# Attention scores with 32 keys in four column tiles, turned by VectorE in 32x32 blocks

## What is computed

```python
scores = einsum('bshc,btc->bsht', q_nope, kv) + einsum('bshr,btr->bsht', q_pe, k_pe)   # 128 + 64 features
scores = softmax(scores / sqrt(192) + causal_mask)       # over the 64 keys t
out = einsum('bsht,btc->bshc', scores, kv)               # kv: 128 features
x = x + out @ (wkv_b, wo folded, per head) + wo_b
```

## Time and profile before

| | |
|---|---|
| median of 3 runs | 1075.35 us (1074.99 to 1075.48) |
| the profiled execution's span | 1073.7 us |
| PE busy | 1052.0 us (98%), mean granted clock 0.999 |
| DVE, ACT, POOL busy | 501.7, 340.6, 280.1 us |
| where stage m's units lie in the span | first scores at 190.6 us, last at 641.1 us |

### The profile page before, as it was taken

One profiled execution on the slowest core, in us unless ns is written; L12 is line 12 of the kernel. 1 busy time (PEld: TensorE's weight loads), 2 busy tenths in 40 slices (PEclk: granted clock), 3 DMA queues, 4 the chain that ended last, 5 costly groups with the idle time before them and its releaser, 6 DMA issues.

```text
span 1073.7 us, 16794 instructions
## 1 busy us (share of the span) xinstructions
PE 1052.0 (98%) x6465; PEld 862.3 (80%) x6465; DVE 501.7 (47%) x914; ACT 340.6 (32%) x630; POOL 280.1 (26%) x329
## 2 busy tenths in 40 slices
PE   6999999999999999999999999999999999999997
PEld 3677786788888888888888888888888888888886
DVE  3666556545555544555555557442522251234114
ACT  3565545423222232123222234342222222223220
POOL 2433362321112111131111312232242123213412
PEclk9999999999999999999999999999999999999999
DMA  9999973200022000220013061600020002000101
GB/s 361 415 418 396 386 274 91 72 20 21 21 64 94 20 12 21 72 96 21 20 50 99 21 206 41 216 1 1 1 76 4 1 1 79 1 1 1 40 1 40
DMA packets 40755, 101.24 MB, mean 94 GB/s; under 512 B 6954, under 2 KB 11077, under 8 KB 36197
## 3 DMA queue, kind: packets, MB, share of 16 engines
q1 hardware_dynamic: 38948, 96.62, 25.3%
q10 hardware_dynamic: 1728, 3.54, 0.8%
HBM read 74.45 MB, written 17.30 MB: 85 GB/s over the span
## 4 chain that ended last, share of the span: by engine, by line
PE 96%; DVE 1%; issue 1%; DMA 1%; POOL 0%; ACT 0%; SPq 0%; DVEq 0%; POOLq 0%; ACTq 0%
PE b_z L44 8%; PE b_z L46 8%; PE b_z L45 8%; PE b_turn L44 5%; PE b_turn L46 4%; PE b_turn L45 4%; PE b_score L44 4%; PE b_score L46 4%; PE b_prob L46 4%; PE b_prob L44 4%; PE b_score L45 4%; PE b_prob L45 4%; PE b_read L46 4%; PE b_read L44 4%; PE b_read L45 4%; PE b_read L623 2%
## 5 line engine op out<-in xcount | busy, mean ns | idle before, releaser
L1516 POOL TENSOR_TENSOR f_hT_lo<-f_h,f_hT_hi 128x512 fp32r<-128x512 f32 x64 | 82.1, 1283 | 241.3 <-ACT f_hT_hi L1571 232.3
L1632 DVE TENSOR_TENSOR f_h<-f_h 128x512 f32<-128x512 f32 x64 | 45.4, 710 | 154.8 <-ACT f_h L1564 154.8
L816 POOL TENSOR_TENSOR m_sc<-m_sc,m_rs 128x1024 f32<-128x1024 f32 x16 | 30.5, 1908 | 248.5 <-DVE m_rs L979 248.5
L44 PE MATMUL b_z<-m_zT_lo,m_wq_hi 128*128 128x512 f32 x192 | 74.9, 390 | 0.3 <-issue 0.3
L46 PE MATMUL b_z<-m_zT_hi,m_wq_hi 128*128 128x512 f32 x192 | 74.7, 389 | 0.0
L45 PE MATMUL b_z<-m_zT_hi,m_wq_lo 128*128 128x512 f32 x192 | 74.7, 389 | 0.0
L987 DVE TENSOR_TENSOR m_x<-b_score,m_x 128x512 f32<-128x512 f32 x32 | 22.1, 691 | 97.3 <-PE b_score L46 97.3
L858 ACT ACTIVATE m_qT<-b_z,m_q_bias 128x512 f32<-128x512 f32 x64 | 44.1, 689 | 71.1 <-PE b_z L46 65.2
L806 POOL TENSOR_TENSOR m_qpe<-m_qpe,m_swapped 128x512 f32<-128x512 f32 x32 | 41.3, 1292 | 79.7 <-DMA m_swapped<-m_by_sin 79.7
L1571 ACT CAST f_hT_hi<-f_h 128x512 fp32r<-128x512 f32 x64 | 39.8, 622 | 52.4 <-DVE f_h L1632 52.4
L879 ACT ACTIVATE m_sc<-m_sc 128x512 f32<-128x512 f32 x32 | 20.2, 632 | 103.0 <-DVE m_sc L971 103.0
(11 more groups left out here) (280 smaller groups left out, 2863.9 us busy)
## 6 DMA issues: line engine op xcount, KB each, us to landing
x_ctx_in<-ctx_rows_dram SPq DMA_DIRECT2D x16, 1024.0 KB, 14.5
x_ctxT<-ctx_turned_dram SPq DMA_DIRECT2D x15, 1024.0 KB, 14.0
m_swapped<-m_by_sin SPq DMA_DIRECT2D x128, 64.0 KB, 2.0
m_raw<-attn_raw_dram SPq DMA_DIRECT2D x6, 768.0 KB, 10.6
m_z_in<-z_scratch SPq DMA_DIRECT2D x4, 1152.0 KB, 5.7
x_x_all<-x_dram SPq DMA_DIRECT2D x16, 256.0 KB, 14.7
m_x<-x_scratch SPq DMA_DIRECT2D x4, 1024.0 KB, 6.3
x_scratch<-m_x SPq DMA_DIRECT2D x4, 1024.0 KB, 4.3
```

The source lines that it names most:

```text
L44: nc.tensor.matmul(out, lh, rl, start=first, stop=False)
L816: q.tensor_tensor(e, e, rs[:].unsqueeze(2).broadcast_to([P, HB, SEQ]), ALU.mult).then_inc(s["normed"], 1)
L1516: q.tensor_tensor(hT_lo[k % 6][:], h[:, k % 2], hT_hi[k % 6][:].bitcast(F32), ALU.subtract).then_inc(s["h_lo"], 1)
L1632: v.tensor_tensor(h[:, k % 2], h[:, k % 2], h[:, k % 2], ALU.mult).then_inc(s["squared"], 1)
```

## The change

Scores are computed for 32 keys at a time in four column tiles of 32 columns, with 128 moving columns where the keys are the first half of a sequence (k = 0) and 64 where they are the second half (k = 1): the first half of the queries sees none of those keys, and this quarter is left out. Tokens are placed so that partition 32c + i of tile t holds token 128c + 32t + i of the group. PE's transposes of scores and of probabilities go; VectorE transposes 32x32 blocks instead, out of PSUM for the scores and from SBUF to SBUF for the probabilities. The mask moves to GpSimd, behind the turn. The maximum and the sum are taken over 32 keys and then joined over the two halves, by two small instructions each. `weigh` has four row tiles of 32 keys, with 256 or 128 moving columns. Loads and stores of latents and residual rows are cut in four, one for each quadrant of partitions.

```diff
     def load_z(sp, g):
-        sp.dma_start(z_in[:, :, 0:ZW], z_t[g]).then_inc(z_loaded, 16)
-        sp.dma_start(z_in[:, :, ZW:ZW + ROPE], z_t[g][:, :, QLR + KVLR:ZW]).then_inc(z_loaded, 16)
+        for c in range(PARTS):
+            sp.dma_start(z_in[part(c), :, 0:ZW], z_t[g, c]).then_inc(z_loaded, 16)
+            sp.dma_start(z_in[part(c), :, ZW:ZW + ROPE], z_t[g, c][:, :, QLR + KVLR:ZW]).then_inc(z_loaded, 16)
...
         def store_x2(g):
             sp.wait_ge(s["x2_done"], T4 * UNITS * (g + 1))
-            sp.dma_start(x2_t[g], x1[:]).then_inc(s["x2_stored"], 16)
+            for c in range(PARTS):
+                sp.dma_start(x2_t[g, c], x1[part(c)]).then_inc(s["x2_stored"], 16)
...
         def load_x1(g):
-            sp.dma_start(x1[:], x1_t[g]).then_inc(s["x1_loaded"], 16)
+            for c in range(PARTS):
+                sp.dma_start(x1[part(c)], x1_t[g, c]).then_inc(s["x1_loaded"], 16)
...
+        def mask(u):
+
+            pool.wait_ge(s["s_turned"], 2 * (u + 1))
+            own = sc[:].rearrange("p (b w n) -> p b w n", b=2, w=3)[:, :, 0::2]
+            q.tensor_tensor(own, own, causal[:].unsqueeze(1).unsqueeze(1).broadcast_to([P, 2, 2, HU * QB]),
+                            ALU.add).then_inc(s["masked"], 1)
...
         def slot(g, n, u):
             if runs(g, n, 1):
+                mask(u - 1)
+            rope_add(u, 0)
+            if runs(g, n, 1):
                 norm(u - 1)
-            rope_add(u)
+            rope_add(u, 1)
             if n == 1:
                 bias_x1(g)
...
+        def turn_scores(u):
 
             dve.wait_ge(s["scored"], u + 1)
+            to = sc[:].rearrange("p (w n) -> p w n", w=6)
             for h in range(2):
+                v.transpose(to[:, :, P // 2 * h:P // 2 * h + P // 2],
+                            b_s[h][:, 0:3 * P].rearrange("p (w n) -> p w n", w=6)).then_inc(s["s_turned"], 1)
+
+        def turn_probs(u):
+
+            dve.wait_ge(s["normed"], u + 1)
+            dve.wait_ge(s["pv"], u)
+            v.transpose(pT[:], sc[:]).then_inc(s["p_turned"], 1)
+
+        def over_keys(u, own, both, op, done, behind):
+
+            v.tensor_reduce(both[:].rearrange("p b w h -> p (b w h)"), sc[:].rearrange("p (n k) -> p n k", k=QB), AX_X, op).then_inc(s[done], 1)
+            dve.wait_ge(s[done], u + 1)
+            v.tensor_copy(own[:, :, 0], both[:, :, 0]).then_inc(s[behind], 1)
+            v.tensor_tensor(own[:, :, 1:3], both[:, :, 1].unsqueeze(2).broadcast_to([P, 2, 2, HU]),
+                            both[:, :, 2].unsqueeze(2).broadcast_to([P, 2, 2, HU]), op).then_inc(s[behind], 1)
 
         def shift(u):
 
+            dve.wait_ge(s["masked"], u + 1)
+            over_keys(u, mx, tops, ALU.max, "maxed", "topped")
+            dve.wait_ge(s["topped"], 2 * (u + 1))
...
             if runs(g, n, 1):
                 shift(u - 1)
+            rotate(n, u, 1)
+            if runs(g, n, 1):
                 invert(u - 1)
-            rotate(n, u, 1)
...
+            if runs(g, n, 1):
+                turn_probs(u - 1)
+                probs(u - 1)
             add(0)
...
+            pe.wait_ge(s["pT_lo"], u + 1)
+            for b in range(2):
                 for n, (kv, p) in enumerate(((kv_hi, pT_lo), (kv_lo, pT_hi), (kv_hi, pT_hi))):
+                    for k in range(2):
+                        cols = slice(2 * P * b + P * k, 2 * P * b + 2 * P)
+                        of = slice(3 * P * b + 2 * P * k, 3 * P * b + 2 * P + P * k)
+                        for c in range(PARTS):
+                            mm = t_.matmul(b_o[c][:, cols], kv[part(c), 2 * b + k], p[part(c), of],
+                                           start=n == 0 and k == 0, stop=n == 2 and k == 1)
...
+            for b in range(2):
+                for k in range(2):
+                    for h in range(2):
+                        for c in range(PARTS):
+                            t_.matmul(b_s[h][part(c), cols(b, k)], keys_all[:, 0, 2 * b + k, c], queries(qT[:, h::2], b, k, c),
+                                      start=b == 0 and k == 0, stop=False)
+            for b in range(2):
+                for k in range(2):
+                    for h in range(2):
+                        for c in range(PARTS):
+                            of = slice(SEQ * h, SEQ * h + SEQ)
+                            mm = t_.matmul(b_s[h][part(c), cols(b, k)], keys_all[of, 1, 2 * b + k, c], queries(qpe[of], b, k, c),
+                                           start=False, stop=b == 1 and k == 1)
```

More of the change, by code:

```diff
@@ L691, in stage_m @@
     by_sin, swapped = low("by_sin", [P, TT]), low("swapped", [P, TT])
-    cos, sin = low("cos", [P, SEQ]), low("sin", [P, SEQ])
-    HB = T4 * HU
-    mx, es, rs = low("mx", [P, HB]), low("es", [P, HB]), low("rs", [P, HB])
+    cos, sin = low("cos", [P, 2 * P]), low("sin", [P, 2 * P])
+    tops, mx, adds, es, rs = (low(n, [P, 2, 3, HU]) for n in "tops mx adds es rs".split())
     x1 = sb("x1", [P, T4, HID])
@@ L795, in gpsimd @@
         pool.wait_ge(s["setup"], 1)
[L796 to L806, removed]
+        for c in range(PARTS):
+            rows = causal[part(c)].rearrange("p (h k) -> p h k", k=QB)
+            q.affine_select(out=rows, in_=rows, compare_op=ALU.is_ge, fill=-BIG, base=0,
+                            pattern=[[0, HU], [-1, QB]], channel_multiplier=1).then_inc(s["consts"], 1)
@@ L827, in groups @@
             slots(pool, slot)
-        return dict(groups=groups, rope_add=rope_add, norm=norm)
+        return dict(groups=groups, rope_add=rope_add, mask=mask, norm=norm)
     def scalar(act):
@@ L861, in probs @@
         def probs(u):
[L862 to L865, removed]
+            act.wait_ge(s["p_turned"], u + 1)
+            act.wait_ge(s["pv"], u)
+            a.copy(pT_hi[:], pT[:]).then_inc(s["pT_hi"], 1)
         def out(u):
@@ L869, in out @@
             act.wait_ge(s["projected"], T4 * u)
[L870 to L873, removed]
+            for c in (2, 3, 0, 1):
+                a.copy(of_part(oT_hi, c), b_o[c][:].rearrange("p (t h q) -> p t h q", t=T4, h=HU)).then_inc(s["oT_hi"], 1)
         def exp(u):
[L877 to L880, removed]
+            act.wait_ge(s["shifted"], u + 1)
+            a.activation(sc[:], sc[:], ACT.Exp, scale=SCALE).then_inc(s["exped"], 1)
         def slot(g, n, u, values_hi):
@@ L1024, in slot @@
                 out(u - 1, 1)
-            mask(u)
+            turn_scores(u)
             if runs(g, n, 1):
@@ L1037, in tables @@
             dve.wait_ge(s["tables"], 48)
-            dve.wait_ge(s["consts"], 2)
+            dve.wait_ge(s["consts"], PARTS)
         return dict(latent=latent, groups=groups, rotate=rotate, invert=invert, probs=probs, out=out,
-                    mask=mask, shift=shift, residual=residual, tables=tables)
+                    turn_scores=turn_scores, turn_probs=turn_probs, shift=shift, residual=residual, tables=tables)
     def tensor(pe):
@@ L1080, in rope_half @@
             mm.then_inc(s["rope_made"], 1)
-        def turn_scores(u):
-            pe.wait_ge(s["masked"], 2 * (u + 1))
-            for half in range(2):
-                turn(b_s[half], lambda k: sc[:, HALF * half + P * k:HALF * half + P * k + P], HB // 4).then_inc(s["s_turned"], 1)
         def q_unit(g, n, u):
@@ L1120, in project, with weigh @@
             mm.then_inc(s["projected"], 1)
-        def weigh(g, u, half, last=False):
+        def weigh(g, u, last=False):
             pe.wait_ge(s["kv_lo"], g + 1)
@@ L1182, in slot @@
                 turn_latent(g + 1, 1)
-            if runs(g, n, 1):
-                turn_probs(u - 1)
             if head and u == 1:
@@ L1195, in slot @@
                     pe.wait_ge(s["zq_lo"], T4 * (g + 2))
-                for half in range(2):
-                    weigh(before(1)[0], u - 1, half)
+                weigh(before(1)[0], u - 1)
             scores(g, u)
@@ L1987, in _ @@
             m["out"](U - 1, 1)
-            m["mask"](U)
+            m["turn_scores"](U)
             m["out"](U - 1, 0)
@@ L2065, in _ @@
             pe.wait_ge(F["s"]["xT_lo"], 4)
-            for half in range(2):
-                m["weigh"](G, U - 1, half)
+            m["weigh"](G, U - 1)
             m["scores"](G, U)
-            m["project"](2, U - 1, 0)
-            m["turn_scores"](U)
-            for i in range(1, 4):
+            for i in range(3):
                 m["project"](2, U - 1, i)
             f["up"](0, 0)
-            m["turn_probs"](U)
             f["up"](0, 1)
-            m["weigh"](G, U, 0, last=True)
+            m["project"](2, U - 1, 3)
             pe.wait_ge(F["s"]["relu"], 2)
-            m["weigh"](G, U, 1, last=True)
+            m["weigh"](G, U, last=True)
             f["up"](0, 2)
```

165 lines of the change are left out of this document (74 added, 91 removed).

## The result

The changed kernel takes 1105.07 us, the median of four runs (1104.57 to 1107.51), beside 1075.41 for the kernel before on the same chip: a ratio of 1.028 (95% interval 1.0266 to 1.0295), 29.7 us slower. 11.6 were forecast. The profiled execution has a span of 1102.8 us, 29.1 more than before.

What follows compares the result with a forecast made beforehand. PE, busy 98% of the span, was taken as the bound. Terms -28.2 - 10.1 + 0 + 33.4 + 6 + 8.1 + 2.4 = 11.6 us more gave 1085.3 profiled, 1087.0 median; own range 1073 to 1101, whole range 1064 to 1111.

Steps and rivals of the forecast that it cites:

- group 0's stop: PE in group 0, slot n=1, behind the late swap DMAs: about 1 us, since there are no project tiles yet.
- PE's stream: PE's own work over 16 units: 38.3 us shorter, 28.2 from turns removed and 10.1 from scores.
- the scores: Score matmuls on PE: 2.30 us a unit for 2.93 if tiles stay independent, 0.63 less, 10.1 in all.
- the weighing: PE's weigh matmuls: no change taken; bounds 5.9 us less or 9.3 more in all.
- The long stops: Slot n=2, groups 1 to 3: PE waits for query copies, mask being behind GpSimd's bias additions; 33.4 us more.
- rival D: VectorE's transposes cost twice an ordinary pass, so turns stay on the path: 6 to 10 us more, 1095; chance 0.12.
- Rival C: DMA pieces land fast, bias begins 2.9 us earlier, and it ends faster than before: 1067.7 us; chance 0.16.
- rival B: Weighing: narrow fp32r matmuls take more passes, 0.22 us a set, 9.3 us more: 1096.3; chance 0.17.
- the stops by the swaps: Slot n=1: eight latent loads delay the swaps, rotate and the residual add; PE stops 8.1 us, between 4 and 14.
- The clock's size: PE at the 1.2 GHz level after each of three stops in slot n=2: 2 us each, 6 in all, bounds 0 and 10.
- The tail: Hand-written part: last unit's chain runs through one transpose and two split weights more before weigh: 2.4 us, between 0 and 4.
- A: Scores on PE: the records' own rate is the bound, 13.9 us dearer instead of 10.1 cheaper: 1106.5; chance 0.14.

Runs made afterwards that it cites:

- all three edits: Changed kernel with bias additions behind norm in slot n=2, latent loads behind slot n=1's swaps, invert and norm ahead of rotate and rope_add: 1045.63 us, ratio 0.9719.

## Why the prediction was right and where it was wrong

**Right: direction, and the mechanism of every term but one (group 0's stop, below).** PE's stream: 2.39 us a slot forecast, 2.38 measured; within it the scores gave 0.50 instead of 0.63, the weighing 0.09 instead of nothing. The long stops: 33.4 forecast, 34.2 measured, in the places named; the link from the mask's place to PE is shown by two kernels that break it differently. `turn_scores` and `turn_probs` on VectorE take 0.58 + 0.54 and 0.98 us, so rival D's price is out:

```profile
L985 DVE STREAM_TRANSPOSE m_pT<-m_sc 128x768 f32<-128x768 f32 x16 | 15.6, 978 | 22.7 <-POOL m_sc L837 22.7
...
L978 DVE STREAM_TRANSPOSE m_sc<-b_turn 128x384 f32<-128x384 f32 x16 | 9.3, 583 | 9.8 <-PE b_free L1184 9.8
L978 DVE STREAM_TRANSPOSE m_sc<-b_free 128x384 f32<-128x384 f32 x16 | 8.6, 540 | 0.0
```

Rival C is out too: the additions begin 12.9 us behind the unit's first score (464.91 to 477.77) instead of 10.1, so 2.8 later, where the sum had 0.9 and C 2.9 earlier. The store takes 2.84 us of the queue and the load is issued 6.2 behind it; in the kernel before 4.4. The three waits are 11.3, 11.9 and 11.0 us for 10.5, 10.7 and 12.2. Measured from the unit's first score, the additions of groups 1 and 2 began 2.4 and 2.8 us later than in the kernel before, not 0.9, and those of group 3 only 0.3 later: its longer load did not come again (GpSimd waits 20.7 us there, 23.0 in group 2). That the sum is only 0.8 off is luck; two misses cancel. Two small slips in the working change nothing here: the chain to the query copies adds up to 477.2, not 477.1, and rival B's own terms, 0.22 for 0.12 in 96 sets, give 9.6, not 9.3.

**Wrong: the stops by the swaps.** This is the step that failed, the term for the latents' load ahead of the swaps: 8.1 us forecast, 18.2 measured, 10 of the 17.5 by which the sum was short. It failed in two places. For group 0 the prediction said "about 1", with "no project tiles yet" as the reason. The missing project tiles are missing cover, not a missing user: PE gets to the fill of the late value weights sooner, and the split that frees its bank stands on VectorE behind the same `rotate`, `invert`, `turn_probs` and `probs`:

```profile
205.16 0.75 DVE L952 SCALAR_TENSOR_TENSOR m_by_sin<-b_read,m_rope_bias,m_sin 128x512 f32<-128x512 f32 x1 [6.25 <-DMA m_swapped<-m_by_sin]
...
212.53 0.68 DVE L1378 TENSOR_TENSOR m_wvo_lo<-b_score,m_wvo_hi 128x512 fp32r<-128x512 f32 x1
```
```profile
213.35 2.05 PE L1343 MATMUL b_score<-m_raw 128*128 128x512 f32 x2 [6.10 <-DVE m_wvo_lo L1378]
```

PE waits 6.1 us for it, where it waited 0.7 before, and the clock adds nearly 2: the two records of L1343 start 0.99 us apart instead of 0.43, and the weighing behind them takes 2.29 us instead of 1.53. That alone is 7.1 instead of 1. For groups 1 and 2 the waits were near the forecast (3.9 and 3.3 us, forecast 3.1 each), but the price of the clock had been given to the long stops only. The six slow matmuls behind each are 1.2 us more, and with the pair ahead of them, 0.56 apart, it is 1.5 to 1.7.

**The clock's size was near for the long stops, and missing for the others.** 6 us were given to the three long stops; their slow matmuls are 29 at 0.2 us more, 5.8, or 7.2 with the pairs at the edges, 0.59 us apart at the start. Counted in the same way, groups 1 and 2 have 3.2, the tail 1.4, and the head 1.9: near 14 in all.

**The tail was mis-sized, 6.9 for 2.4.** The two stops were named; their waits are 2.3 and 1.7 us, and there is one of 0.3. The slow matmuls add 1.4, the end behind the last matmul 0.5. The rest, 0.7, was not traced. The last two stops fell to a reordering on VectorE alone, so they were not the price of the longer chain but of its place.

**Rivals.** The result lies at A's number, 1106.5, by a different road: A's mechanism is refuted by the scores' 2.43 us and by the kernel with the quarter kept. A time that agrees with a rival is no sign for it; the stage it speaks of has to be looked at.

## What to carry to other kernels

- When work moves to another engine, write down what stands in front of its new place in each slot, and read the waits of *those* instructions. A wait of 20 us that costs nothing becomes the bound once something wanted early is queued behind it; here four additions moved were worth 33 us, and order alone turned 2.8% slower into 3.3% faster.
- Where there is less work on the bounding engine (the first units, the tail), there is less cover. Price a delay there at its full length, and give every stop of some 3 us its slow matmuls.
- Two causes of one stop don't add. Take both away before the account is closed.

## What the runs showed of the hardware

**Narrow tiles run denser than any row of before.** In the second part of the scores 64 records on eight tiles start within 0.98 us, 15 ns from one to the next; the narrow ones among them run faster still:

```profile
434.29 0.24 PE L1184 MATMUL b_turn<-m_qpe,m_keys 64*32 64x64 f32 x4
...
434.40 0.41 PE L1184 MATMUL b_turn<-m_qpe,m_keys 64*32 64x128 f32 x5
```

The four groups from the one to the other, of which the first is shown, are 16 records in 0.11 us, 7 ns each. The Trainium skill ("TensorE: Matmul & The Clock Gate", section "Wait — 56ns, not 53.3ns?") says that start-to-start never drops below about 25 ns; across tiles it does here. The part as a whole takes 0.98 where columns alone would give 0.66, and I have not found out what holds it. Nor is it steady: of the first 15 units 13 take 0.98 to 1.00 and two take 1.20 and 1.23, while with all columns each of the 15 takes 1.09.

**A stop of 2 to 4 us can already cost clock, and its length doesn't tell how much.** Behind the stop of 3.3 us at 453 in slot n=1 six matmuls start 0.43 to 0.41 us apart. Behind three stops of 11 to 12 us it is 5, 12 and 12. The tail's two stops are 2.3 and 1.7 us long in most of the kernels here, and 0.43 us apart behind them start 5 and 0 matmuls in the changed kernel, 7 and 6 in the one with the additions moved, 0 and 4 in the one with the loads moved, 7 and 3 in the one with all three edits. Nor need the clock fall at once: with the mask on VectorE, PE runs at 0.23 us a matmul for 1 us behind the stop of 3.8 us (360.28) before eight come slow. So one trace with a stop and no slow matmul is no sign that the stop is free.

**Small VectorE instructions take longer beside GpSimd's additions.** In the kernel with the mask on VectorE the sum's two small instructions fall together with GpSimd's additions (471.48 to 476.5). The two of the maximum, outside of it, are the measure:

```profile
466.72 0.17 DVE L988 COPY m_mx<-m_tops 128x8 f32<-128x8 f32 x1
466.80 0.17 DVE L989 TENSOR_TENSOR m_mx<-m_tops 128x16 f32<-128x16 f32 x1
...
474.56 0.75 DVE L988 COPY m_es<-m_adds 128x8 f32<-128x8 f32 x1
475.23 1.33 DVE L989 TENSOR_TENSOR m_es<-m_adds 128x16 f32<-128x16 f32 x1
```

0.17 becomes 0.75 and 1.33 us; an addition of GpSimd takes 1.26. The reduction ahead of them keeps its 0.94. The Trainium skill ("SBUF — State Buffer", section "Who interferes with whom") says that VectorE and GpSimd hold a shared port pair in turn, each for a whole instruction, and that on VectorE a copy can contend for it, an instruction with two inputs in SBUF does, and a reduction never does. These rows agree, and so does the kernel with the additions behind `norm`: there the two of the sum lie ahead of the additions (472.18 to 472.43) and take 0.17 and 0.17. How long the delay is depends on how they meet: in groups 1 and 3 of the kernel with the mask on VectorE the copy takes 0.63 and 0.78 us, and the instruction behind it 0.16.
